# Reordering the tail of an attention and mixture-of-experts kernel: output projection directly after its normalization tile, routing logits in one step

## The reference, cut to what matters

```python
qkv = layernorm(x) @ Wqkv                       # 16 heads of 16
num = exp(rot(q) @ rot(k).T * scale)            # with rotary embedding, causal
den = sum(exp(q @ k.T * scale))                 # without it, over all keys
x = x + (num / den @ v) @ Wout + bout
xf = layernorm(x)
logits = xf @ Wr                                # 8 experts
prob = trunc(softmax(top2(logits)))             # not 0 only where a weight is 1
x = x + relu(xf @ Ws1)**2 @ Ws2 + sum_e prob_e * expert_e(xf)
```

## Time and profile before

| | us |
|---|---|
| median of 3 runs | 1656.03 (1655.13 to 1657.16) |
| profiled execution | 1656.43 |
| its span in the trace | 1654.7 |
| ScalarE busy | 1587.1 (96%) |
| TensorE busy | 1483.4 (90%) |
| VectorE busy | 851.1 (51%) |
| GpSimd busy | 521.9 (32%) |
| last exponential ends, start of the tail | about 1625.3 |

### The profile page before, as it was taken

The page is one execution under the profiler, slowest core; times in us unless marked ns, Lnnn a source line. Parts: engine busy times, 40 slices in busy tenths (PEclk is TensorE's granted clock), DMA queues, the critical chain, the costliest instruction groups (busy, mean ns, idle before and its releaser), DMA issues.

```text
span 1654.7 us, 25505 instructions
## 1 busy us (share of the span) xinstructions
PE 1483.4 (90%) x8226; PEld 572.7 (35%) x8226; DVE 851.1 (51%) x1961; ACT 1587.1 (96%) x2641; POOL 521.9 (32%) x863
## 2 busy tenths in 40 slices
PE   4888989999999989999899899989999999999986
PEld 2322333333333333333343343333333333333334
DVE  5334434765346653566445653566434665356416
ACT  2999999999999999999999999999999999999992
POOL 3324133432234322333332323334133432234310
PEclk8998999999999999999999999999999999999998
DMA  5532233331434313333234234333243421433300
GB/s 160 156 99 80 86 106 115 120 101 55 131 115 131 111 44 122 122 124 106 80 118 124 94 96 131 100 121 97 73 131 115 141 93 42 135 113 103 115 27 26
DMA packets 95389, 172.05 MB, mean 104 GB/s; under 512 B 15696, under 2 KB 82256, under 8 KB 83152
## 3 DMA queue, kind: packets, MB, share of 16 engines
q1 hardware_dynamic: 94656, 169.55, 32.7%
q10 hardware_dynamic: 592, 0.79, 0.2%
HBM read 111.55 MB, written 58.72 MB: 103 GB/s over the span
## 4 chain that ended last, share of the span: by engine, by line
ACT 88%; PE 6%; issue 4%; DVE 1%; DMA 1%; DVEq 0%; ACTq 0%; POOL 0%; SPq 0%; POOLq 0%
ACT scores L541 57%; ACT probs L551 27%; ACT probs L553 4%; PE scores L599 2%; PE y_ps L628 1%; PE side L638 1%; PE scores L606 1%; PE scores L657 0%; DMA x_in<-in_L_attn_x 0%; PE side L657 0%; PE scores L647 0%; PE scores L773 0%; ACTq L315 0%; PE scores L784 0%; DVEq L894 0%
## 5 line engine op out<-in xcount | busy, mean ns | idle before, releaser
L541 ACT ACTIVATE scores<-scores 128x1024 f32<-128x1024 f32 x1024 | 1067.6, 1122 | 16.8 <-PE scores L599 16.5
L599 PE MATMUL scores<-stack 96*128 96x512 bf16 x2048 | 585.3, 385 | 77.8 <-ACT scores L541 40.1
L551 ACT ACTIVATE probs<-scores 128x1024 f32<-128x1024 f32 x512 | 491.7, 1111 | 2.8 <-PE scores L606 1.7
L606 PE MATMUL scores<-stack 96*128 96x512 bf16 (+3 forms) x1536 | 335.0, 330 | 46.7 <-ACT scores L541 37.6
L438 POOL TENSOR_SCALAR_AFFINE_SELECT probs<-probs 128x256 f32<-128x256 f32 (+1 forms) x640 | 240.8, 403 | 387.7 <-ACT probs L551 219.0
L628 PE MATMUL y_ps<-probs,v_sb 128*32 128x512 f32 (+3 forms) x3072 | 331.8, 504 | 5.1 <-POOL probs L438 5.1
L599 PEld LDWEIGHTS scores<-stack 96*128 96x128 bf16 x2048 | 152.6, 97 | 486.1 <-ACT scores L541 209.9
L541 ACT ACTIVATION_READ_ACCUMULATOR scores<-scores 128x1 f32 x1024 | 300.5, 293 | 0.0
L448 POOL TENSOR_TENSOR parts<-rest,parts 128x512 bf16<-128x512 f32 x124 | 143.2, 1155 | 292.8 <-DVE parts L961 292.8
L606 PEld LDWEIGHTS scores<-stack 96*128 96x128 bf16 x1536 | 116.9, 98 | 300.1 <-ACT scores L541 154.5
L446 POOL TENSOR_TENSOR rot<-raw,cos_sb 128x512 f32<-128x512 f32 x62 | 89.3, 1440 | 390.2 <-DVEq L971 390.2
(11 more groups left out here) (141 smaller groups left out, 1062.0 us busy)
## 6 DMA issues: line engine op xcount, KB each, us to landing
stack<-qk_parts SPq DMA_DIRECT2D x756, 128.0 KB, 2.6
qk_parts<-parts SPq DMA_DIRECT2D x127, 384.0 KB, 2.6
out<-x_mid SPq DMA_DIRECT2D x32, 256.0 KB, 2.9
x_in<-in_L_attn_x SPq DMA_DIRECT2D x7, 1024.0 KB, 5.3
stack<-qk_parts SPq DMA_DIRECT2D x18, 64.0 KB, 2.3
x_in<-in_L_attn_x SPq DMA_DIRECT2D x2, 512.0 KB, 4.4
probs<-in_L_attn_Wqkv SPq DMA_DIRECT2D x1, 512.0 KB, 5.7
cos_sb<-in_cos SPq DMA_DIRECT2D x1, 512.0 KB, 6.5
```

Source lines behind the costliest of these rows:

```text
L541: nc.scalar.activation(src, src, ACT.Exp, scale=SCALE, accum_out=den[:, g % 2, i, j:j + 1]).then_inc(exp_done, 1)
L551: nc.scalar.activation(probs[:, chunk % 2, j, :], src, ACT.Exp, scale=SCALE).then_inc(exp_done, 1)
L599: mm = nc.tensor.matmul(tile[:, half * HALF:(half + 1) * HALF], q[:, j, i * P:(i + 1) * P], k[:, j, half * HALF:(half + 1) * HALF], start= ...
L606: mm = nc.tensor.matmul(tile[:, col:col + n], k[:, h, i * P:(i + 1) * P], q[:, h, q0:q0 + n], start=True, stop=True)
```

## The change

The list of tiles gets another order, and `logits_t` and `logits` become one tile. Its product has the tokens as stationary operand (a 128x128 piece of `xn2t`) and the 8 columns of `wr_sb` as the moving one: 4 blocks times 2 halves of the features, 8 matmuls. VectorE copies 128x32 logits at once. The list before and after, from `norm` 1 on:

| | order |
|---|---|
| before | norm 1, up 2, logits_t 1, acc 0, acc 1, up 3, down 2, t2 0, t2 1, logits 1, down 3, logits_t 0, up 0, up 1, logits 0, down 0, down 1, routed |
| after | norm 1, up 2, acc 0, acc 1, logits 1, up 3, down 2, down 3, t2 0, t2 1, logits 0, up 0, routed, up 1, down 0, down 1 |

```diff
-END_TILES = [("norm", 0), ("acc", 2), ("acc", 3), ("t2", 2), ("t2", 3), ("norm", 1), ("up", 2),
-             ("logits_t", 1), ("acc", 0), ("acc", 1), ("up", 3), ("down", 2), ("t2", 0), ("t2", 1),
-             ("logits", 1), ("down", 3), ("logits_t", 0), ("up", 0), ("up", 1), ("logits", 0), ("down", 0),
-             ("down", 1), ("routed", 0)]
+END_TILES = [("norm", 0), ("acc", 2), ("acc", 3), ("t2", 2), ("t2", 3), ("norm", 1), ("up", 2), ("acc", 0), ("acc", 1),
+             ("logits", 1), ("up", 3), ("down", 2), ("down", 3), ("t2", 0), ("t2", 1), ("logits", 0), ("up", 0),
+             ("routed", 0), ("up", 1), ("down", 0), ("down", 1)]
@@ tensor program
-                elif what == "logits_t":
+                elif what == "logits":
                     pe.wait_ge(end_taken, END_TILES.index(("t2", 2 * t + 1)) + 1)
-                    for k in range(KC):
-                        for j in range(2):
-                            mm = nc.tensor.matmul(side[32 * j:32 * j + 32, 0:2 * P], wr_sb[:, k, :],
-                                                  xn2t[:, k, (4 * t + 2 * j) * P:(4 * t + 2 * j + 2) * P],
-                                                  start=k == 0, stop=k == KC - 1, tile_position=(0, 32 * j),
-                                                  skip_group_check=True)
-                elif what == "logits":
-                    pe.wait_ge(end_taken, END_TILES.index(("logits_t", t)) + 1)
-                    for i in range(2):
-                        mm = nc.tensor.transpose(side[:, i * P:(i + 1) * P], logits_t[:, i * P:(i + 1) * P], ident[:, :])
+                    for i in range(NB // 2):
+                        for k in range(KC):
+                            mm = nc.tensor.matmul(side[:, i * E:(i + 1) * E], xn2t[:, k, (4 * t + i) * P:(4 * t + i + 1) * P],
+                                                  wr_sb[:, k, 0:E], start=k == 0, stop=k == KC - 1)
@@ vector program
-                elif what == "logits_t":
-                    nc.vector.tensor_copy(logits_t[0:P // 2, :], side[0:P // 2, 0:2 * P]).then_inc(end_taken, 1)
                 elif what == "logits":
                     half = slice(t * NB // 2, (t + 1) * NB // 2)
-                    nc.vector.tensor_copy(logits[:, half, :].rearrange("p (j i) e -> p i j e", i=2),
-                                          side[:, 0:2 * P].rearrange("p (i j e) -> p i j e", i=2, j=4)[:, :, 0:2, 0:E]
+                    nc.vector.tensor_copy(logits[:, half, :].rearrange("p i e -> p (i e)"), side[:, 0:E * NB // 2]
                                           ).then_inc(end_taken, 1)
```

## The result

The changed kernel takes 1660.68 us (median of 9 runs, 1659.27 to 1661.84) against 1656.1 for the kernel before in the same runs. The ratio is 1.0023, 95% interval 1.0015 to 1.0032. So it is slower, clear of noise: by 4.6 us in the medians, by 3.8 by the ratio, with 2.5 to 5.3 as the interval.

What follows compares the result with a forecast made beforehand. ScalarE's exponentials carry 88% of the chain but stay untouched, so the tail, bound in turn by VectorE and TensorE, decides. Walked at 1.2 GHz, the steps move the span from 1654.7 to 1661.5: 1656.03 + 6.8 = 1662.8 us, range 1658.0 to 1664.5.

Steps and rivals of the forecast that it cites:

- rival 2: The clock rises during logits 0: early at 1646.1, 1658.1 us (0.12); late near 1649.5, 1660.0 to 1661.5 (0.14).
- rival 3: Weight loads of the new logits tile keep 0.11 us a pair at 1.2 GHz: 1.75 us less, 1661.0; chance 0.12.
- one sign of being wrong: The prediction said it would be wrong if the granted clock is at 2.4 GHz after 1641.
- Step 1: acc 0 and acc 1 no longer stand behind logits_t 1, so VectorE's additions come earlier: a gain of 1.65 us.
- The fourth rival: The change does not do what it says: acc 0 was held by its operand, not logits_t 1; called excluded.
- Step 2: logits 1, up 3 and down 2 on TensorE, 3.5 us, are covered by VectorE's chain: cost nothing.
- Step 3: down 3, waiting for the square of up 3, holds back t2 0 and t2 1: a loss of 2.3 us there.
- Step 4: logits 0 as one tile of 16 load and matmul pairs: 1.76 to 4.1 us, taken as 3.5 at 1.2 GHz.
- Step 5: routed ahead of up 1 makes TensorE wait for VectorE's weights: a new stop of 2 us; branch no longer last.
- The last write: At the end of the span: starts 0.14 us after the last addition, lands 2.2 later, plus 0.15 for SyncE.
- Which clock: TensorE's work from 1640.65 on has gaps, so 1.2 GHz was taken throughout; called the least certain choice.
- Rival 1: The clock stays at 2.4 GHz over TensorE's pause before down 3: span 1655.0, time 1656.3, no change; chance 0.07.

Runs made afterwards that it cites:

- e2: The kernel before with only acc 0 and acc 1 moved ahead of logits_t 1; 1654.76 us, ratio 0.9992.
- e12: e5 with the count (routed) at the end of the list and idle products only ahead of down 3; 1656.18 us, ratio 1.0003.
- e10: e6 with the idle products that e8 has, 4 ahead of norm 1 and 6 ahead of t2 0; 1653.38 us, ratio 0.9987.
- e7: e2 with 6 idle TensorE products, whose result nobody reads, ahead of t2 0; 1652.08 us, ratio 0.9982.
- e8: e7 with 4 more idle products ahead of norm 1, behind the last score tile; 1653.01 us, ratio 0.9977.
- e5: The changed kernel with idle products in TensorE's two pauses, 11 ahead of down 3 and 3 ahead of routed; 1658.62 us, ratio 1.0010.
- e11: e5 with down 3 behind t2 1, idle products 6 ahead of t2 0 and 3 ahead of routed; 1656.57 us, ratio 1.0003.
- e1: The changed kernel with its new logits tile at the old places, logits 1 ahead of acc 0 and the count last; 1657.49 us, ratio 1.0018.
- e3: The changed kernel with down 3 put back behind the transposes t2 0 and t2 1; 1660.40 us, ratio 1.0029.
- e6: The changed kernel with down 3 back behind t2 1 and the count back at the end, keeping the new tile; 1658.14 us, ratio 1.0007.
- e4: The changed kernel with the count of tokens (routed) put back at the end of the list; 1658.85 us, ratio 1.0016.
- e9: e6 with each product of a logits tile streaming 128 columns instead of 8; 1655.81 us, ratio 0.9996.

## Why the prediction was right

The measured 1660.68 lies in the range of 1658.0 to 1664.5 and on the forecast side of no change, 2.1 us below 1662.8. It does not lie in the narrower forecast of 1662 to 1663.6, which had a chance of 0.5. It lies where the late rise of rival 2 (1660.0 to 1661.5) and rival 3 (1661.0) stand, and neither is what happened. And one sign of being wrong that the prediction names did occur: the granted clock was at 2.4 GHz after 1641, from 1645.4 to 1648.8. The direction and the two stops were right for the reasons given; that the number came so close is in part luck. The tail was to grow from 29.4 us to 36.2, by 6.8; in the profiles it grew to 33.0, by 3.6. The medians differ by 4.6, and of the 1.0 more that lies in them no term of the sum speaks. Of the 3.2 us that the forecast tail was too long, 0.9 are gone by the start of logits 0, 1.7 are logits 0, 0.8 are up 0 and 0.4 stand behind it; the last write then took 0.6 more than its term. Point by point:

- **Step 1, the projection moves up: right, and the clock added to it.** 1.65 us were worked out, 1.5 came out in e2's median. In the changed kernel's profile it is 2.4, since the clock rose at 4.7 us behind the last exponential instead of 7.1. The fourth rival, that acc 0 was held by its operand, is out: in e2 it starts right behind up 2.
- **Step 2, logits 1 hidden: right.** The tile took 1.85 us and TensorE stood for 4.97 behind it and its two neighbours.
- **Step 3, down 3 ahead of the transposes: right.** The wait for the square is the row of 1641.43; 4.6 us of pause were expected. logits 0 starts 19.0 us behind the last exponential, the walk had 19.9. At one clock this move costs 1.5 us (e12's tail less that of e10 and less the 1.37 that the filling ahead of norm 1 gives, e7 to e8: 27.80 - 24.97 - 1.37; the start of logits 0 from e5 to e11 also moves by 1.4).
- **Step 4, the price of the new tile: the pace was right, its clock was not.** Double the pace at half the clock was chosen between 0.11 and 0.26 us a pair; e1 shows 0.204 and e3 0.2125. So rival 3 is refuted. The rule of the Trainium skill ("TensorE: Matmul & The Clock Gate", section "LDWEIGHTS (loading the stationary operand)") is columns / 1.2, without a word on the clock. It fits the pace of these float32 pairs at 2.4 GHz, 0.111, and not at 1.2. But in the profiled execution the clock rose at 1645.4, ahead of the tile, which took 1.78 us instead of 3.5. This is the largest term that was wrong, 1.7 us too large.
- **Step 5, the count ahead of up 1: right.** The stop is 1.78 us for 2 expected; the branch is no longer last. up 0 ahead of it was taken 1.14 us after its start and not 1.95, by the same clock.
- **The last write** was issued at about 1657.1 and the span ended 2.9 later; the sum had 2.35. That is the one term that was too small. The last two output writes, with the issue in ns and, below, the time to landing:

```profile
L382 SPq DMA_DIRECT2D out<-x_mid x2: 372/586/800, 1655.8 to 1657.1; - x2
...
DMA to landing us min/median/max: 2.6/2.9/3.2
```

- **Which clock: wrong up to the second stop, right behind it.** The prediction calls it its least certain choice. The profile has a mixture that no case had: 2.4 GHz for logits 0 and up 0, earlier than rival 2 had it, then a fall at the second stop and 1.2 GHz for the three tiles behind it, as in the forecast. Rival 2 gave 1658.1 with the clock up to the end, the forecast 1662.8 with it down, and the time lies between.
- **Rival 1, the clock stays up over the pause:** refuted for the kernel as it is (fall at 1638.6). e5 forced it by filling. Its tail of 29.4 equals that of the kernel before, as the rival's 1655.0 against 1654.7 said; its median of 1658.62 lies 2.3 above the rival's 1656.3.

So the cause is a sum. By the medians, the moved projection gives 1.5 us from the kernel before (e2). The new tile then takes 3.1 (e6), of which 0.35 are its own (e10, from the profiles) and the rest comes through the clock. down 3 early takes 1.0 more (e4 against e6), the early count 2.0 (after against e4). In the other order these two are 0.4 and 2.5 (e3). By the ratios the four parts are -1.3, 2.5, 1.5 and 1.2, so the split is known to a microsecond at best. Among these, the intervals that don't overlap are those of the changed kernel and e4 against e2, and of e3 against e6. What holds without the split is that the changed kernel loses by new stops and by work at 1.2 GHz: e5, with the clock held up, takes 3.6 us off its tail and 2.1 off its median. What remains open is what exactly decides when the clock rises.

## What to carry to other kernels

When two in-order engines share a list of tiles, walk it for the tile behind which others stand whose operands are ready: a tile moved up is free only if its own operand is there too, and a product that waits for the other engine's long chain (down 3) must not stand ahead of one that feeds that engine (1.4 to 1.5 us here at one clock). In a tail that is full of short pauses, look at the granted clock before the instruction counts. Ten idle products in the pauses (e8) gave 2 us more than the best order alone (1.4 in the tail), and an order that was 3 us better on paper gave nothing, with a clock that stayed down for 13.6 us in its profile (e3).

## What was unexpected in the hardware

- The clock rose while TensorE stood still: at 1645.4 in the changed kernel, between transposes that ended at 1645.2 and a tile that began at 1646.06. And it stayed at 1.2 GHz through 8.5 us of work without a gap in e6 (1642.94 to 1651.4), where the kernel before needed 6.1 and 6.0 and the changed one 3.7 for its first rise (1628.04 to 1631.75).
- 16 weight loads of 128 columns, and not what streams behind them, set the time of a tile: streaming 128 columns instead of 8 behind each made it 1.95 us instead of 1.85 at 2.4 GHz and 3.60 instead of 3.55 at 1.2 (e9, e6).
- The last exponential of one and the same loop lay between 1624.8 and 1628.4 in fourteen profiles. A difference of 1 us between two single profiles of this kernel means nothing unless it is taken from a common point.
